# Four cross-attention layers in one kernel: constant rows replicated by transfer, preparation steps in a new order, epsilon as a tile, no shift column

## The chip, the cores and the metric

The kernel runs on one core of one Trainium2 chip. The metric is device time in microseconds, as the median of several executions. TensorE (PE), VectorE (DVE), ScalarE (ACT) and GpSimd (POOL) compute; SyncE (SP) issues all DMA transfers.

## The reference

Input are x (64 batches, 128 tokens, 256 features), a context ctx (64, 128, 128) and a side input (64, 128, 128), all float32. Four residual layers follow each other:

```
L0: x = x + softmax((x Wq + bq)(ctx Wk + bk)' / 16) (ctx Wv + bv) Wo + bo
L1: t = x + cross(ln(x), ln(ctx)) + cross(ln(x), ln(side));  x = t + ln(t) fc_W + fc_b
L2: p = x + softmax over the queries((x Wq + bq)(ctx Wk + bk)' / 16) (ctx Wv + bv);  x = ln(p) gamma + beta
L3: as L0, with its own weights
```

ln(x) is (x - mean) * (var + eps)^(-1/2) over the features, with eps 1e-5 in L1 and 1e-6 in L2; in L1 it has gains and offsets (g1, b1 for queries, g2, b2 for keys).

## The kernel before

**Groups.** The work is cut into 32 groups of two batches. Each group goes through some ninety steps such as `hi_L0`, `Q_L0`, `S_L0`, `max_L0`, `exp_L0`, `PT_L0`, `O_L0`, `OUT_L0`, `out_L0`, `stats_ln1`. A step belongs to one engine and handles a whole group. Below, `Q_L0(1)` is step `Q_L0` of group 1.

**Order.** A table sets the order on every engine. `STARTS` gives each step a number, `COMES` an offset for each group; `PREPARATIONS` gives numbers to the one-time work on the weights. `timetable()` sorts all of it, and each engine issues its own steps in that order, each behind its semaphore waits. Nothing overtakes.

**Preparation.** Projections are folded once: for each attention `a` (L0, L1a, L1v, L3) PE forms `M_a` = Wq Wk' and `N_a` = Wv Wo (`products`), `m_a` from the query bias (`query_bias`) and `n_*` from the value and output biases (`output_bias`). ACT and DVE cut M and N into a high and a low fp32r part (`M_hi`, `M_lo`). A constant row (an output bias, beta, gamma, a key gain) comes as one row of the tile `rows` on a single partition, and is spread over the partitions by a product with `ones_row` (L355, L395, L411, L419, L441): ten such products in all. ACT copies results out of PSUM into `bias_*` and `gamma_row`; DVE multiplies the keys' weights by the gain in PSUM (L869).

**Layer norm.** DVE computes `stats` (L909), `mean_var` (L915) and `var_eps` = var + eps (L919). POOL raises it to -1/2 (`rstd`, L1076). DVE forms `shift` = -mean * rstd (L943), and POOL computes x * rstd + shift (`norm_*`, L1082). For the norm before fc neither shift nor normalised x is made.

**PSUM.** Eight banks are handed out by `seats()` in the order of the table, always the one whose last user is emptied first.

Of the kernel before, what the change touches and what calls it, by code (L numbers as in the profile page):

```python
# [78 lines left out]
PREPARED = {"keys_L1": [("gain_L1a", "gained_L1a"), ("gain_L1v", "gained_L1v")],  # L79
            "products_L0": [("M_L0", "M_lo_L0"), ("N_L0", "N_lo_L0")],  # L80
            "vectors_L0": [("m_L0", "m_col_L0"), ("n_L0", "bias_L0")],
            "products_L1": [("M_L1a", "M_lo_L1a"), ("N_L1a", "N_lo_L1a"), ("M_L1v", "M_lo_L1v"), ("N_L1v", "N_lo_L1v")],
            "vectors_L1": [("m_L1a", "m_col_L1a"), ("m_L1v", "m_col_L1v"), ("n_L1", "bias_L1")],
            "fc": [("n_fc", "bias_fc"), ("mean_fc", "centred_fc")],
            "L2": [("M_L2", "M_lo_L2"), ("k_L2", "k_bias2"), ("n_L2", "bias_L2v")],
            "products_L3": [("M_L3", "M_lo_L3"), ("N_L3", "N_lo_L3")],
            "vectors_L3": [("m_L3", "m_col_L3"), ("n_L3", "bias_L3"), ("gamma", "gamma_row")]}
# [24 lines left out]

def seats(table):

    at = {(name, g): n for n, (_, g, name) in enumerate(table)}
    held, seat = [None] * BANKS, {}
    for _, g, name in table:
        uses = PREPARED.get(name, []) if g < 0 else [(name, EMPTIED_BY[name])] if name in EMPTIED_BY else []
        for use, emptied in uses:
            n = min(range(BANKS), key=lambda b: -1 if held[b] is None else held[b][2])  # L120
            assert held[n] is None or held[n][2] <= at[name, g], f"no bank for {use} {g}"
            seat[use, max(g, 0)] = n, held[n] and held[n][:2]
            held[n] = emptied, max(g, 0), at[name, g] if g < 0 else at[emptied, g]
    return seat


def build(nc, ins, out):
    with ExitStack() as stack:  # L128
# [109 lines left out]
        for engine, signals in SIGNALS.items():  # L238
# [1 line left out]
            for n, name in enumerate(name for _, _, p in table for name in signals.get(p, [])):  # L240
# [988 lines left out]
```

## Time and profile before

| what | value |
|---|---|
| median of 3 runs | 613.43 us (612.94 to 614.08) |
| profiled execution, its own time | 613.34 us |
| span of the profile, first to last instruction | 611.5 us |
| granted PE clock, mean | 0.993 |
| PE busy | 582.3 us, 95% |
| DVE busy | 537.5 us, 88% |
| POOL busy | 520.0 us, 85% |
| ACT busy | 431.5 us, 71% |

All times in the rows are counted from the start of the span. 1.84 us of the profiled execution lie outside it. A matmul on float32 leaves two records in the trace, a matmul on fp32r one. Busy time of PE is of pipelined matmuls, so its share does not say how fast they follow each other; the starts in the timeline do.

### The profile page before, as it was taken

To read this page: it belongs to the slowest core of one execution; us is meant where nothing else is said; L and a number is where in the kernel's file an instruction comes from. 1 tells how busy PE (TensorE), PEld (TensorE's weight loads), DVE (VectorE), ACT (ScalarE), POOL (GpSimd) and SP (SyncE) were. 2 spreads that over 40 slices of the span, in tenths; PEclk is the share of its full clock that TensorE was granted. 3 is DMA by queue.
4 is the path that set the end of the run, shared out by engine and by line. 5 is a ranking of instruction groups with operands and counts; after the bars stand their busy time and mean duration, and the time that the engine had idled before them with its cause. 6 is when DMAs were issued, how large, how long until landed. Compare 5 with 4: busy or idle time off the path is not lost. (4 is left out here: it accounts for less than half of the span.)

```text
span 611.5 us, 16892 instructions
## 1 busy us (share of the span) xinstructions
PE 582.3 (95%) x4872; PEld 567.7 (93%) x4872; DVE 537.5 (88%) x1685; ACT 431.5 (71%) x1473; POOL 520.0 (85%) x694
## 2 busy tenths in 40 slices
PE   4889999899999999999999999999999999999985
PEld 4778999899999999999999999999999899999974
DVE  1457789999999999999999999999999999989993
ACT  2546967777777778778777777877876788677443
POOL 3268887898999999999999999999999999867763
PEclk9998999999999999999999999999999999999999
DMA  8512211003222211122222221112333020000012
GB/s 274 217 62 70 82 48 46 3 1 96 80 78 80 78 56 51 54 80 79 78 80 79 79 79 53 48 60 78 114 104 114 17 89 28 18 3 19 19 35 70
DMA packets 28076, 42.80 MB, mean 70 GB/s; under 512 B 2513, under 2 KB 19793, under 8 KB 27985
## 3 DMA queue, kind: packets, MB, share of 16 engines
q1 hardware_dynamic: 27986, 41.72, 20.6%
q8 instruction: 41, 0.67, 0.5%
q14 instruction: 49, 0.40, 0.2%
HBM read 33.32 MB, written 8.39 MB: 68 GB/s over the span
## 5 line engine op out<-in xcount | busy, mean ns | idle before, releaser
L720 ACT ACTIVATE prob_L<-bank,neg_max_L 128x128 f32<-128x128 f32 x320 | 114.1, 379 | 70.1 <-DVE neg_max_L L952 69.7
L1082 POOL TENSOR_SCALAR xhat_ln<-x,rstd_ln,shift_ln 128x256 f32<-128x256 f32 x128 | 71.1, 564 | 14.0 <-issue 7.4
L652 ACT ACTIVATE oT_hi_L<-bank 128x256 fp32r<-128x256 f32 (+1 forms) x128 | 55.9, 460 | 34.4 <-PE bank L476 34.4
L720 ACT ACTIVATION_READ_ACCUMULATOR prob_L<-bank,neg_max_L 128x1 f32 x320 | 69.1, 216 | 0.0
L952 DVE TENSOR_REDUCE neg_max_L<-bank 128x2 f32<-128x256 f32 (+1 forms) x128 | 59.0, 477 | 11.5 <-PE bank L470 11.1
L652 ACT ACTIVATE xT_hi_L<-bank 128x512 fp32r<-128x512 f32 (+1 forms) x96 | 59.5, 620 | 7.4 <-PE bank L448 7.1
L854 DVE TENSOR_TENSOR oT_lo_L<-bank,oT_hi_L 128x256 fp32r<-128x256 f32 (+1 forms) x128 | 58.7, 478 | 2.9 <-ACT oT_hi_L L652 2.8
L1076 POOL TENSOR_TENSOR rstd_ln<-var_eps_ln,minus_half 128x2 f32<-128x2 f32 x64 | 45.3, 708 | 12.6 <-DVE var_eps_ln L919 7.4
L1116 POOL TENSOR_TENSOR xT_lo_L<-x_in,xT_hi_L 128x512 fp32r<-128x512 f32 x32 | 41.0, 1282 | 12.2 <-ACT xT_hi_L L652 12.2
L652 ACT ACTIVATE probT_L<-bank 128x256 f32<-128x256 f32 (+1 forms) x96 | 47.4, 495 | 4.3 <-PE bank L454 4.1
L985 DVE TENSOR_TENSOR x<-bank,x_bias 128x512 f32<-128x512 f32 x64 | 43.8, 685 | 6.5 <-PE bank L489 4.3
L919 DVE TENSOR_SCALAR var_eps_ln<-mean_var_ln 128x2 f32<-128x2 f32 x64 | 46.7, 730 | 2.2
L909 DVE BATCH_NORM_STATS2 stats_ln<-x 128x6 f32<-128x256 f32 x128 | 47.7, 414 | 0.9
L454 PE MATMUL bank<-ident,prob_L 128*128 128x128 f32 x256 | 44.0, 274 | 1.9 <-DVE xT_lo_L L854 0.9
L854 DVE TENSOR_TENSOR xT_lo_L<-bank,xT_hi_L 128x512 fp32r<-128x512 f32 x64 | 43.5, 679 | 1.0 <-ACT xT_hi_L L652 1.0
L487 PE MATMUL bank<-N_hi_L,oT_hi_L 128*128 128x256 f32 x128 | 41.2, 322 | 3.1 <-issue 1.5
L803 ACT ACTIVATE prob_L<-prob_L,inv_total_L 128x128 f32<-128x128 f32 x128 | 42.2, 441 | 1.5 <-DVE inv_total_L L959 1.5
L1156 POOL TENSOR_TENSOR x_res<-x_res,bias_L 128x512 f32<-128x512 f32 x32 | 41.1, 1283 | 2.5
L470 PE MATMUL bank<-ctx_in,qT_L 128*128 128x128 f32 x256 | 39.1, 276 | 3.2 <-issue 2.1
L1154 POOL TENSOR_TENSOR x_res<-xhat_ln,gamma_row 128x512 f32<-128x512 f32 x32 | 41.3, 1291 | 0.0
L1139 POOL TENSOR_TENSOR x_bias<-x,bias_fc 128x512 f32<-128x512 f32 x32 | 41.2, 1289 | 0.0
L1132 POOL TENSOR_TENSOR x_bias<-x,bias_L 128x512 f32<-128x512 f32 x32 | 41.2, 1287 | 0.0
(217 smaller groups left out, 2390.9 us busy)
## 6 DMA issues: line engine op xcount, KB each, us to landing
x_in<-in_x SPq DMA_DIRECT2D x32, 512.0 KB, 4.2
ctx_in<-in_ctx SPq DMA_DIRECT2D x32, 256.0 KB, 4.3
out<-y SPq DMA_DIRECT2D x32, 256.0 KB, 2.2
side_in<-in_side SPq DMA_DIRECT2D x32, 128.0 KB, 2.5
WqT_L<-in_L_WqT SPq DMA_DIRECT2D x3, 256.0 KB, 4.3
Wo_L<-in_L_Wo SPq DMA_DIRECT2D x2, 256.0 KB, 4.7
WkT_L<-in_L_WkT SPq DMA_DIRECT2D x3, 128.0 KB, 4.1
WvT_L<-in_L_WvT SPq DMA_DIRECT2D x2, 128.0 KB, 4.0
```

Source lines behind the costliest of these rows:

```text
L454: last = tr(block(bank, b), src[:, b, :], ident[:])
L652: activation(to, of, ACT.Copy).then_inc(done[step], 1)
L720: last = activation(at(prob[k], g)[:, b, :], block(bank, b), ACT.Exp, bias=at(neg_max[k], g)[:, b:b + 1], accum_out=at(total[k], g)[:, b:b ...
L803: last = activation(p[:, b, :], p[:, b, :], ACT.Copy, scale=at(inv_total["L1"], g)[:, b:b + 1])
L854: dve.tensor_tensor(to, of, hi.bitcast(F32), ALU.subtract).then_inc(done[step], 1)
L909: last = dve.bn_stats(st[:, n, :], tile)
L919: dve.tensor_scalar(at(var_eps[k], g)[:], mv[:, :, 1], eps, None, ALU.add).then_inc(done[f"var_{k}"], 1)
L952: dve.tensor_reduce(at(neg_max[k], g)[:], scores, AX.X, ALU.max, negate=True).then_inc(done[f"max_{k}"], 1)
L985: dve.tensor_tensor(flat(at(to, g)), bank_of(use, g)[:], flat(at(add, g)), ALU.add).then_inc(done[step], 1)
L1076: pool.tensor_tensor(at(rstd[k], g)[:], at(var_eps[k], g)[:], minus_half[:, 0:n], ALU.pow).then_inc(done[f"rstd_{k}"], 1)
L1082: last = pool.tensor_scalar(at(to, g)[:, n, :], tile, at(rstd[k], g)[:, n:n + 1], at(shift[k], g)[:, n:n + 1], ALU.mult, ALU.add)
L1154: pool.tensor_tensor(at(x_res, g)[:], at(xhat["ln2"], g)[:], every(gamma_row), ALU.mult).then_inc(done["x_gamma"], 1)
```

## The change

1. **Constant rows by transfer.** Each constant row is read by a transfer that writes it to all 128 partitions (`replicated` in the SP program): ten transfers of 128 KB (64 KB for the two gains) in place of the one for `rows`. The ten products with `ones_row` go. DVE adds the row when it takes the bias out of PSUM (`bias_plus`); POOL adds rows that belong together (`rows_L1`, `rows_L3`) and multiplies the keys' weights by the gain (`gained`, before on DVE). Copies of `m_col` and `k_bias2` move from ACT to DVE.
2. **First weights first.** WqT and WkT of L0 are the first two transfers. Each pair of weights has a semaphore of its own, so `M_L0` waits for two transfers, where it waited for four.
3. **Preparation in single steps.** What were 14 entries in `PREPARATIONS` are now 84, each for one engine, with new numbers. L3's preparation (2794 to 3293 before) now stands at 940 to 1060, ahead of `PT_L0(0)`.
4. **Epsilon as a tile.** `var_eps` is a tensor_tensor add of a tile `epsilon` where it was a tensor_scalar add of an immediate.
5. **No shift.** POOL computes (x - mean) * rstd from `mean_var` and `rstd`. The 96 `shift` instructions of DVE go, and with them the hop POOL to DVE to POOL.

The order of all group steps other than `shift` is the same as before.

```diff
-PREPARATIONS = {"load_first": -50, "constants": -40, "keys_L0": 81, "products_L0": 284, "vectors_L0": 406,
-                "load_rest": 506, "keys_L1": 516, "products_L1": 626, "fc": 666, "L2": 968, "vectors_L1": 1238,
...
+PREPARATIONS = {"load_qk_L0": -50, "load_cols": -49, "load_vo_L0": -48, "load_rows_L0": -47, "constants": -40, "scaled": -39, "M_L0": 100,
...
-            def load_first():
-                sp.dma_start(cols[:], ins["cols"].rearrange("p (n t) -> p n t", t=T)).then_inc(weights["vectors"], 16)
-                sp.dma_start(rows[:], ins["rows"].rearrange("(o n) d -> o n d", o=1)).then_inc(weights["vectors"], 16)
-                weights_of("L0")
+            def replicated(to, r, what):
+                n, width = ROWS.index(r), to.shape[1]
+                sp.dma_start(to[:], ins["rows"][n:n + 1, 0:width].to_broadcast([P, width])).then_inc(weights[what], 16)
...
+            def product_M(a):
+                def of():
                     w = stage[a]
-                    pe.wait_ge(weights[a], ATTENTION_WEIGHTS)
+                    pe.wait_ge(weights[f"{a}_qk"], TWO)
                     if a in LN_KEYS:
                         prepared(pe, f"gained_{a}")
...
-                terms += [(ones_row[:], row(r)) for r in extra]
...
+            def bias_plus(key, to, use, added):
+                dve.tensor_tensor(to[:], bank_of(use)[:, 0:D], added[:], ALU.add).then_inc(done[key], 1)
...
-                dve.tensor_scalar(at(var_eps[k], g)[:], mv[:, :, 1], eps, None, ALU.add).then_inc(done[f"var_{k}"], 1)
+                if g == 0:
+                    prepared(dve, "constants")
+                dve.tensor_tensor(at(var_eps[k], g)[:], mv[:, :, 1], epsilon[eps][:, 0:len(tiles)], ALU.add).then_inc(done[f"var_{k}"], 1)
...
-            def shift_of(k):
-                def of(g):
-                    dve.wait_ge(done[f"rstd_{k}"], g + 1)
-                    earlier(dve, f"norm_{k}", g, len(shift[k]))
-                    dve.scalar_tensor_tensor(out=at(shift[k], g)[:], in0=at(mean_var[k], g)[:, :, 0], scalar=-1.0,
-                                             in1=at(rstd[k], g)[:], op0=ALU.mult, op1=ALU.mult).then_inc(done[f"shift_{k}"], 1)
...
+            def gained(a):
+                def of():
+                    pool.wait_ge(weights[f"{a}_qk"], TWO)
+                    pool.wait_ge(weights[f"gain_{a}"], ONE)
+                    w = stage[a]["WkT"]
+                    pool.tensor_tensor(w[:], w[:], gain[a][:].unsqueeze(1).to_broadcast([P, T, P]), ALU.mult).then_inc(done[f"gained_{a}"], 1)
...
-                    last = pool.tensor_scalar(at(to, g)[:, n, :], tile, at(rstd[k], g)[:, n:n + 1], at(shift[k], g)[:, n:n + 1],
-                                              ALU.mult, ALU.add)
+                    last = pool.tensor_scalar(at(to, g)[:, n, :], tile, at(mean_var[k], g)[:, n, 0:1], at(rstd[k], g)[:, n:n + 1],
+                                              ALU.subtract, ALU.mult)
```

**SP, just ahead of the first context.** `ctx_in` is the tile that `hi_ctx(0)` on ACT and `S_L0(0)` on PE wait for. Before, it is the 24th transfer:

```order
L318 DMA fcW<-in_fc_W 128x2x256
L306 DMA WqT_L<-in_L_WqT 128x2x256
L306 DMA WkT_L<-in_L_WkT 128x2x128
L306 DMA WvT_L<-in_L_WvT 128x2x128
L306 DMA Wo_L<-in_L_Wo 128x2x256
L328 DMA ctx_in<-in_ctx 128x512
```

Now it is the 33rd (`row_L_bo`, `row_L_b` and `gamma_row` are the replicated rows of L3):

```order
L463 DMA WvT_L<-in_L_WvT 128x2x128
L463 DMA Wo_L<-in_L_Wo 128x2x256
L467 DMA row_L_bo<-in_rows 128x256
L467 DMA row_L_b<-in_rows 128x256
L467 DMA gamma_row<-in_rows 128x256
L509 DMA ctx_in<-in_ctx 128x512
```

All ten new transfers stand ahead of it, and the one for `rows` is gone: nine more. One of the ten (`row_L_bo` of L0) stands even ahead of the first `x_in`, which stays the seventh transfer.

**ACT, around `hi_ctx(0)`** (`ctxT_hi<-ctx_in`). Before, it stands behind everything that ACT does for L1v:

```order
L652 ACTIVATE M_L1v<-bank 128x256
L664 ACTIVATE M_hi_L1v<-bank,scaled_cols 128x128
L665 ACTIVATE M_hi_L1v<-bank,scaled_cols 128x128
L652 ACTIVATE N_L1v<-bank 128x256
L674 ACTIVATE N_hi_L1v<-bank,cols 128x256
L652 ACTIVATE ctxT_hi<-ctx_in 128x256
```

Now L1v stands behind it:

```order
L867 ACTIVATE N_hi_L1a<-bank,cols 128x256
L835 ACTIVATE ctxT_hi<-ctx_in 128x256
L835 ACTIVATE M_L1v<-bank 128x256
L849 ACTIVATE M_hi_L1v<-bank,scaled_cols 128x128
L850 ACTIVATE M_hi_L1v<-bank,scaled_cols 128x128
L835 ACTIVATE N_L1v<-bank 128x256
```

So PE's `m_L1v`, which needs the copy `M_L1v`, now comes behind the landing of the first context.

**PE, ahead of `PT_L0(0)`** (`prob_L_0`). Before, the products of L1's output bias with their two rows stand there:

```order
L395 MATMUL bank<-Wo_L1a,rep_bv_L1a 128x256 x2
L395 MATMUL bank<-N_L1a,rep_b_L1a 128x256
L395 MATMUL bank<-Wo_L1v,rep_bv_L1v 128x256 x2
L395 MATMUL bank<-N_L1v,rep_b_L1v 128x256
L395 MATMUL bank<-rows,ones_row 128x256 x2
L454 MATMUL bank<-ident,prob_L_0 128x128 x2
```

Now L3's four products (M, N, m, n) are the last ahead of it:

```order
L539 MATMUL bank<-WkT_L,WqT_L 128x128 x4
L550 MATMUL bank<-Wo_L,WvT_L 128x256 x2
L566 MATMUL bank<-scaled_cols,WkT_L 128x1 x2
L566 MATMUL bank<-scaled_cols,M_L 128x1 x2
L582 MATMUL bank<-Wo_L,rep_bv_L 128x256 x2
L636 MATMUL bank<-ident,prob_L_0 128x128 x2
```

## Rows read from the trace of the kernel before

**Rows 1.** The page: busy time, share of the span, instructions.
```profile
PE 582.3 (95%) x4872; PEld 567.7 (93%) x4872; DVE 537.5 (88%) x1685; ACT 431.5 (71%) x1473; POOL 520.0 (85%) x694
```

**Rows 2.** Windows: busy us and records by engine, granted clock, DMA share, GB/s.
```profile
300.00:350.00 50.00, 50.00 (x437) 49.84 (x437) 47.88 (x155) 37.80 (x131) 47.44 (x62) 1.00 0.23 73
...
13.24:18.20 4.96, 4.52 (x31) 4.11 (x31) 1.97 (x7) 2.45 (x8) 0.88 (x4) 1.00 1.07 385
...
29.85:33.26 3.41, 3.41 (x9) 2.29 (x8) 0.00 (x0) 0.00 (x0) 0.89 (x1) 0.50 0.09 36
...
50.30:53.72 3.42, 3.42 (x17) 3.42 (x17) 1.36 (x3) 0.77 (x3) 3.23 (x7) 0.50 0.55 208
```

**Rows 3.** Waits of PE over the span: who for whom, us, times, longest.
```profile
PE bank L487 <- DVE oT_lo_L L854: 3.4, 4, 1.4
...
PE bank L463 <- DVE xT_lo_L L854: 2.0, 3, 1.1
```

**Rows 4.** Timeline of PE: start, us, instructions, and idle before them.
```profile
7.39 2.04 PE L366 MATMUL bank<-WkT_L,WqT_L 128*128 128x128 f32 x8 [7.39 <-DMA Wo_L<-in_L_Wo]
...
32.49 1.49 PE L395 MATMUL bank<-rows,ones_row 1*128 1x256 f32 x4
33.91 0.44 PE L454 MATMUL bank<-ident,prob_L 128*128 128x128 f32 x2
...
42.46 1.06 PE L366 MATMUL bank<-WkT_L,WqT_L 128*128 128x128 f32 x8
...
44.03 0.47 PE L487 MATMUL bank<-N_hi_L,oT_hi_L 128*128 128x256 f32 x1
...
46.80 0.61 PE L381 MATMUL bank<-scaled_cols,WkT_L 128*128 128x1 f32 x4 [0.33 <-DVE M_lo_L L873]
...
50.24 1.17 PE L476 MATMUL bank<-probT_L,ctx_in 128*128 128x128 f32 x4
51.06 0.56 PE L463 MATMUL bank<-xT_hi_L,M_hi_L1a 128*128 128x256 f32 x1
```

**Rows 5.** Groups of DVE by line: busy us, mean ns, idle before.
```profile
L919 DVE TENSOR_SCALAR var_eps_ln<-mean_var_ln 128x2 f32<-128x2 f32 x64 | 46.7, 730 | 2.2
...
L943 DVE SCALAR_TENSOR_TENSOR shift_ln<-mean_var_ln,rstd_ln 128x2 f32<-128x2 f32 x64 | 15.4, 240 | 1.9 <-POOL rstd_ln L1076 1.9
...
L919 DVE TENSOR_SCALAR var_eps_keys<-mean_var_keys 128x4 f32<-128x4 f32 x32 | 14.9, 465 | 1.1
...
L943 DVE SCALAR_TENSOR_TENSOR shift_keys<-mean_var_keys,rstd_keys 128x4 f32<-128x4 f32 x32 | 6.4, 201 | 0.0
```

**Rows 6.** Line L919: duration ns min/median/max, first and last start.
```profile
L919 DVE TENSOR_SCALAR var_eps_ln<-mean_var_ln x64: 168/664/1393, 41.5 to 594.4; 128x2 f32<-128x2 f32 x64
```

**Rows 7.** Timelines of POOL and DVE around two short DVE instructions.
```profile
341.25 1.28 POOL L1116 TENSOR_TENSOR xT_lo_L<-x_in,xT_hi_L 128x512 fp32r<-128x512 f32 x1
...
341.28 1.27 DVE L919 TENSOR_SCALAR var_eps_ln<-mean_var_ln 128x2 f32<-128x2 f32 x1
...
36.58 1.26 POOL L1116 TENSOR_TENSOR xT_lo_L<-x_in,xT_hi_L 128x512 fp32r<-128x512 f32 x1
...
36.73 1.14 DVE L943 SCALAR_TENSOR_TENSOR shift_keys<-mean_var_keys,rstd_keys 128x4 f32<-128x4 f32 x1
```

**Rows 8.** Timeline of DVE, 42 to 50 us.
```profile
42.51 0.68 DVE L943 SCALAR_TENSOR_TENSOR shift_ln<-mean_var_ln,rstd_ln 128x2 f32<-128x2 f32 x1 [0.74 <-POOL rstd_ln L1076]
...
49.12 0.67 DVE L854 TENSOR_TENSOR xT_lo_L<-bank,xT_hi_L 128x512 fp32r<-128x512 f32 x1
```

**Rows 9.** The first group's timeline: SP issues its context, POOL computes lo_L0(0).
```profile
12.82 0.47 SPq L328 DMA_DIRECT2D ctx_in<-in_ctx  x1
...
10.97 1.27 POOL L1116 TENSOR_TENSOR xT_lo_L<-x_in,xT_hi_L 128x512 fp32r<-128x512 f32 x1 [7.27 <-ACT xT_hi_L L652]
```

**Rows 10.** Tile WqT_L, 0 to 4 us: issue to landing.
```profile
DMA to landing us min/median/max: 2.7/2.7/2.7
```

**Rows 11.** Tile ctx_in, 0 to 26 us: issue to landing of three.
```profile
DMA to landing us min/median/max: 5.2/6.1/6.9
```

More of the change, by code:

```diff
@@ L77 @@
               "S_L3": "exp_L3", "PT_L3": "pT_L3", "O_L3": "oT_lo_L3", "OUT_L3": "out_L3"}
[L79 to L87, printed above, removed]
@@ L88 @@
-SMALL = [f"{what}_{k}" for what in ("stats", "mean", "var") for k in ("keys", "ln1", "lnf", "ln2")] + ["x_gamma"]
-SIGNALS = {"TensorE": {"keys_L1": ["gain_L1a", "gain_L1v"], "products_L0": ["M_L0", "N_L0"], "vectors_L0": ["m_L0", "n_L0"],
[13 rows of a table removed]
+EMPTIED_BY |= {"m_L0": "m_col_L0", "n_L0": "bias_L0", "m_L1a": "m_col_L1a", "m_L1v": "m_col_L1v", "n_L1": "bias_L1", "n_fc": "bias_fc",
+               "mean_fc": "centred_fc", "M_L2": "M_lo_L2", "k_L2": "k_bias2", "m_L3": "m_col_L3", "n_L3": "bias_L3"}
+EMPTIED_BY |= {f"{w}_{a}": f"{w}_lo_{a}" for w in "MN" for a in ATTENTIONS}
@@ new lines @@
+OF_ENGINE = {"TensorE": [f"{w}_{a}" for w in "MNm" for a in ATTENTIONS] + ["n_L0", "n_L1", "n_L3", "n_fc", "mean_fc", "M_L2", "k_L2"],
+             "ScalarE": ([f"{w}_hi_{a}" for w in "MN" for a in ATTENTIONS] + [f"M0_{a}" for a in ("L1a", "L1v", "L3")]
+                         + ["N0_L1a", "N0_L1v", "gained_fc", "F_hi", "M_hi_L2", "Wv2_hi"]),
+             "VectorE": (["scaled"] + [f"{w}_lo_{a}" for w in "MN" for a in ATTENTIONS] + [f"m_col_{a}" for a in ATTENTIONS]
+                         + ["bias_L0", "bias_L1", "bias_L3", "bias_fc", "centred_fc", "F_lo", "M_lo_L2", "k_bias2", "Wv2_lo"]),
+             "GpSimd": ["constants", "gained_L1a", "gained_L1v", "rows_L1", "rows_L3"] + [f"rep_{a}" for a in ATTENTIONS + ["fc"]]}
@@ L106, in timetable @@
+SMALL = [f"{what}_{k}" for what in ("stats", "mean", "var") for k in ("keys", "ln1", "lnf", "ln2")] + ["x_gamma", "zeroed"]
 def timetable():
-    table = [(STARTS[name] + COMES[g], g, name) for name in STARTS for g in range(GROUPS)]
-    table += [(PREPARATIONS[name], -1, name) for name in PREPARATIONS]
+    table = [(times[g], g, name) for name, times in STARTS.items() for g in range(GROUPS)]
+    table += [(time, -1, name) for name, time in PREPARATIONS.items()]
     return sorted(table)
@@ L117, in seats @@
     for _, g, name in table:
[L118 to L123, printed above, removed]
+        if name in EMPTIED_BY:
+            n = min(range(BANKS), key=lambda b: -1 if held[b] is None else at[held[b]])
+            assert held[n] is None or at[held[n]] <= at[name, g], f"no bank for {name} {g}"
+            seat[name, g] = n, held[n]
+            held[n] = EMPTIED_BY[name], g
     return seat
@@ L188, in build @@
             layer_buffers(k)
-        stats, mean_var, var_eps, rstd, shift = ({} for _ in range(5))
+        stats, mean_var, var_eps, rstd = ({} for _ in range(4))
         for k, n in {"keys": A["L1"] * GROUP, "ln1": GROUP, "lnf": GROUP, "ln2": GROUP}.items():
@@ L212, in build @@
             Wv2 = sb("Wv2", [P, D], where=staging)
-            rows = sb("rows", [1, len(ROWS), D], where=staging)
+            rows = {r: sb(f"row_{r}", [P, D], where=staging) for r in ("L0_bo", "L1a_bo", "L1v_bo", "L3_bo", "L3_b1", "fc_bias")}
+            gain = {a: sb(f"gain_{a}", [P, P], where=staging) for a in ("L1a", "L1v")}
             for a in ATTENTIONS + ["fc"]:
@@ L237, in build @@
         times = {}
[L238 removed]
+        for engine, names in OF_ENGINE.items():
             raised = stack.enter_context(nc.semaphore(f"prepared_{engine}"))
[L240 removed]
+            for n, name in enumerate(name for _, g, name in table if g < 0 and name in names):
                 done[name], times[name] = raised, n + 1
@@ L413, in fc, with of @@
-            def fc():
-                pe.wait_ge(weights["fc"], FC_WEIGHTS)
+                def of():
+                    prepared(pe, "scaled")
+                    pe.wait_ge(weights[f"{a}_qk"], TWO)
+                    if a in LN_KEYS:
+                        prepared(pe, f"gained_{a}")
+                    bank = bank_for(pe, f"m_{a}")
+                    terms = [(stage[a]["WkT"][:, h, :], col(f"{a}_bq", h, scaled_cols)) for h in range(T)]
+                    if a in LN:
+                        prepared(pe, f"M0_{a}")
+                        terms += [(M0[a][:, t, :], col(f"{a}_b1", t, scaled_cols)) for t in range(T)]
+                    for n, (stationary, moving) in enumerate(terms):
+                        last = mm(bank[:, 0:1], stationary, moving, start=n == 0, stop=n == len(terms) - 1)
+                    last.then_inc(done[f"m_{a}"], 1)
@@ new lines, in query_bias, with output_bias, of @@
+                return of
+            def output_bias(key, attentions):
+                def of():
+                    bank = bank_for(pe, f"n_{key}")
+                    terms = []
+                    for a in attentions:
+                        prepared(pe, f"rep_{a}")
+                        pe.wait_ge(weights[f"{a}_vo"], TWO)
+                        terms += [(rep[a]["bv"][:, h, :], stage[a]["Wo"][:, h, :]) for h in range(T)]
+                        if a in LN_KEYS:
+                            prepared(pe, f"N0_{a}")
+                            terms += [(rep[a]["b2"][:], N0[a][:])]
+                    for n, (stationary, moving) in enumerate(terms):
+                        last = mm(bank[:, 0:D], stationary, moving, start=n == 0, stop=n == len(terms) - 1)
+                    last.then_inc(done[f"n_{key}"], 1)
+                return of
@@ L415, in fc, with n_fc @@
+            def n_fc():
+                pe.wait_ge(weights["fc"], ONE)
                 prepared(pe, "rep_fc")
                 bank = bank_for(pe, "n_fc")
-                terms = [(rep["fc"]["bv"][:, t, :], fcW[:, t, :]) for t in range(T)] + [(ones_row[:], row("fc_bias"))]
-                for n, (stationary, moving) in enumerate(terms):
-                    last = mm(bank[:, 0:D], stationary, moving, start=n == 0, stop=n == len(terms) - 1)
+                for t in range(T):
+                    last = mm(bank[:, 0:D], rep["fc"]["bv"][:, t, :], fcW[:, t, :], start=t == 0, stop=t == T - 1)
@@ L1067, in keys_L1, with replicated, of @@
-            def keys_L1():
-                replicated("L1a", "L1a_bv")
-                replicated("L1v", "L1v_bv")
+            def replicated(a):
+                def of():
+                    pool.wait_ge(weights["cols"], ONE)
+                    for t in range(T):
+                        last = pool.tensor_copy(rep[a]["bv"][:, t, :], col("fc_b" if a == "fc" else f"{a}_bv", t).to_broadcast([P, P]))
+                    if a in LN_KEYS:
+                        last = pool.tensor_copy(rep[a]["b2"][:], col(f"{a}_b2").to_broadcast([P, P]))
+                    last.then_inc(done[f"rep_{a}"], 1)
+                return of
@@ L1071, in rstd_of, with rows_L3 @@
+            def rows_L3():
+                pool.wait_ge(weights["rows_L3"], THREE)
+                pool.tensor_tensor(rows["L3_bo"][:], rows["L3_bo"][:], rows["L3_b1"][:], ALU.add).then_inc(done["rows_L3"], 1)
             def rstd_of(k, used_by):
                 def of(g):
+                    if g == 0:
+                        prepared(pool, "constants")
                     pool.wait_ge(done[f"var_{k}"], g + 1)
```

345 lines of the change are left out of this document (184 added, 161 removed), and 203 rows, old and new, of tables (COPIES, PREPARATIONS, SIGNALS, STARTS).

## The prediction, made before the changed kernel ran

> **What bounds the kernel now.** I read the page first. PE is busy 95%, DVE 88%, POOL 85% [rows 1], so three engines are close together and shares alone decide nothing. Next I took windows. In the middle of the run PE is busy 50.00 of 50 us, DVE 47.88, POOL 47.44 [rows 2]: PE never waits there. The 437 records in 50 us are one every 114 ns. The order of the group steps is unchanged, so the middle (about 100 to 450 us) can't get shorter by anything that DVE or POOL save. The time is PE's work, plus what PE loses at the start, in the fill of the pipeline and in the last groups. The list of PE's waits says who is late after the start: the two largest entries are DVE's `oT_lo` (3.4 us) and `xT_lo` (2.0 us) [rows 3]. The timeline of PE gives the landmarks of the start: first product at 7.39 us, behind the landing of the fourth weight tile; first softmax transposed (`PT_L0(0)`) at 33.91; first `Q_L1` at 51.06 [rows 4].
>
> **The change, part by part.**
>
> *First product.* `M_L0` now waits for the first two transfers alone. The first issue is at about 0.7 us, the next half a microsecond later; the tile WqT_L0 landed 2.7 us after its issue [rows 10]. So PE starts at about 0.7 + 0.5 + 2.7 = 3.9 us, 3.5 us earlier. I do not count that as gain: ACT's first steps need the first `x_in`, still the seventh transfer, and what PE does next is gated by POOL and by a transfer.
>
> *Gain multiply.* `gained_L1a` goes from DVE to POOL, behind `lo_L0(0)`, which ended at 10.97 + 1.27 = 12.24 [rows 9]. With about 0.3 us for the row put ahead of `x_in`, and 0.65 for a product half the size of that one, `M_L1a` starts near 13.2. PE, done with L0 by then, idles some 2.5 us. It hides in the 3.5 us gained.
>
> *Context.* This is the new gate. The 24th transfer was issued at 12.82 us [rows 9], that is one each 0.526 us from 0.7 on; the 33rd comes at 0.7 + 32 x 0.526 = 17.5. It landed 5.2 us after issue in a busy stretch [rows 11], where the DMA engines moved 385 GB/s at full share [rows 2]; a transfer into quiet queues took 2.7 [rows 10]. The ten rows add 8 x 128 + 2 x 64 = 1152 KB, at 385 GB/s 3 us; by bytes the old landing of 12.82 + 5.2 = 18.0 becomes 21.0. Bounds: 20.2 (quiet) and 22.7 (busy). I take 21.5, since the queues fall neither quiet nor stay full. The price of reading one row 128 times is in no row; see the rivals. `hi_ctx(0)` on ACT waits for it, the copy `M_L1v` is queued behind, and PE's `m_L1v` behind that: with two ACT steps of about 0.4 us, 22.4. PE will idle there about 4 us.
>
> *From there to `PT_L0(0)`.* PE has 68 records to issue: `m_L1v` 8, `n_L1` 12, `n_fc` and `mean_fc` 8, `M_L2` and `k_L2` 12, `S_L0(0)` 4, L3's four products 24. L3's M and N took 44.03 - 42.46 = 1.57 us for 12 records [rows 4], 0.13 each; 68 make 8.9, so 31.3. DVE's `m_col_L3` and `max_L0(0)` and ACT's two exponentials follow, some 1.3: 32.6. PE's clock was granted at half, 1.2 for 2.4 GHz, for 3.41 us of this stretch before and for 3.42 us from 50.30 on [rows 2], each costing 1.7 us of PE's work; two idles of 2.5 and 4 us just ahead make one such piece as likely as not, so half of 1.7. `PT_L0(0)` at 33.5: **gain 0.4** (bounds -3 and +3.5).
>
> The Trainium skill (TensorE: Matmul & The Clock Gate, Part 1: The HAM clock gate) says that the clock follows how busy PE has recently been. By it the longer idle would make the half clock certain, and the sum above 0.85 us worse.
>
> *PT to Q_L1(0).* Before, L3's preparation lay inside: 1.57 us at 42.46, and from 46.80 less its wait of 0.33 to 50.24, that is 3.77 [rows 4]. All 5.3 us leave this stretch. But PE can't use it all: `Q_L1(0)` needs `lo_L1(0)` of DVE, which ended at 49.12 + 0.67 = 49.79 [rows 8], so PE was the later by 1.27. Beyond that DVE's own chain must get shorter. It loses the `shift` at 36.73, 1.14 us long [rows 7], and the one at 42.51, 0.68 plus 0.74 of waiting for POOL [rows 8]: 2.56, of which `oT_lo` can use about 2.1, as ACT's `oT_hi` comes next. **Gain 1.3 + 2.1 = 3.4** (bounds 1.3 and 5.3).
>
> *Ten row products.* Two of them, as four records, took 33.91 - 32.49 = 1.42 us at half clock for the most part [rows 4]. Ten would be about 5 us of PE; seven lie ahead of `PT_L0(0)`, L3's three between the landmarks, and both stretches are costed above as a whole. No separate gain.
>
> *Shift.* DVE loses 96 instructions, 15.4 + 6.4 = 21.8 us [rows 5], 0.7 per group. In the middle they cover nothing, PE being late. If PE's idle in late groups came all from DVE, the gain were the 5.4 us of the two entries [rows 3]; I take 2.0, since several of those waits are the last groups' own latency, where PE, ACT and DVE hand over in turn. **Gain 2.0** (bounds 0 and 5.4).
>
> *Epsilon.* `var_eps` of 128x2 took 730 ns on average, 168 at least [rows 5, 6]. The timelines say why: at 341.28 it ran until 342.55, when POOL's tensor_tensor of 341.25 ended at 342.53 [rows 7]. It stands still while POOL runs. Will an add of two SBUF tiles escape? The removed `shift` is such an instruction, two SBUF tiles in, 128x4 out, and at 36.73 it ran until 37.87, when POOL's tensor_tensor of 36.58 ended at 37.84 [rows 7]. The same wait to 30 ns. So I cost this edit at **nothing** (bounds: 0 and 61.6 - 96 x 0.168 = 45 us of DVE time). POOL's side is covered too: `norm` keeps its size.
>
> The Trainium skill (SBUF — State Buffer, Who interferes with whom) speaks against this edit: a DVE instruction with two SBUF inputs contends with a GpSimd instruction that reads SBUF, as one in a 2-port mode does. The trace agrees for POOL's tensor_tensor, 1.14 and 1.27 us.
>
> *Copies to DVE, `rows_*` to POOL.* Below half a microsecond each, all in the start, in the terms above.
>
> Sum: 0.4 + 3.4 + 2.0 = 5.8 us. Span 611.5 - 5.8 = 605.7; with the 1.84 outside, 607.5. The profiled execution (613.34) is as good as the median (613.43), so **607.5 us** is the median too.
>
> **Rivals.**
>
> 1. *The epsilon add does escape POOL's lock* (15%). For it: the mean `shift` took only 240 and 201 ns [rows 5], so most did not wait. Against: the one at 36.73 did [rows 7], and `var_eps` stands in the table where POOL runs its long adds. DVE would shed up to 45 us; in the middle nothing follows, in fill and end the waits for DVE shrink by 3 more: 604.5.
> 2. *DVE does not hold the fill* (12%). PE keeps the 3.5 us of the earlier start or all 5.3 of L3's block: 607.5 less 5.3 - 3.4 = 1.9 and about 2 of the start: 603.6.
> 3. *Gain given back* (15%). What PE gains before 51 us it waits for later in the fill, where DVE and POOL are behind it: only the 2.0 and the 0.4 stay: 611.0.
> 4. *Slower: the first context comes late* (10%). The replicated rows all read one line of memory 128 times and stand ahead of `ctx_in(0)` in SP's queue. If they take three times what their bytes say, 6 us more, `ctx_in(0)` lands at 27.5, and PE idles 10 us behind `hi_ctx(0)`; every microsecond goes straight to `PT_L0(0)`. The forecast's 5.8 is gone once the landing is later than 27.3; with a second piece at half clock, 615. For it: the order above. Against: no transfer in rows 10 and 11 took over 6.9.
>
> **How the numbers follow.** The forecast has 48%, the rivals 15, 12, 15 and 10. Its own range is 605 to 610. A measurement of this kernel tells 0.2%, 1.2 us, from no change, so faster is below 612.2. The forecast, rivals 1 and 2 and most of rival 3 are faster: 84%. Rival 3's rest and the best of rival 4 are the same, 6%; slower 10%. The 80% range cuts rival 4 and the lower end of rival 2: 603.3 to 612.0.
>
> **What the profile after will show.** First matmul near 3.9 us; an idle of PE of about 4 us before `m_L1v`, ended by ACT and behind it by the landing of `ctx_in`; `PT_L0(0)` near 33.5; `Q_L1(0)` near 47.3; in the middle PE busy 50 of 50 as before and DVE down by about 2 us in 50; the `var_eps` group with a mean still over 0.5 us and single ones that end with a POOL tensor_tensor. The prediction is wrong if the `ctx_in` landing is far from 21.5, if `var_eps` shrinks to 0.2 us, or if the distance from `PT_L0(0)` to `Q_L1(0)` stays near 17.2.

## The result, and the profile after

The changed kernel takes 712.57 us (median of 4 runs, 711.19 to 713.51) against 613.66 us for the kernel before on the same chip: a ratio of 1.161, 95% interval 1.1585 to 1.1638. I had forecast 607.5 us, in a range of 603.3 to 612.0. The prediction was wrong, by 105 us, and in its direction.

The page of the kernel after, its part 1, which answers to [rows 1]:

```profile
PE 608.7 (86%) x4852; PEld 586.8 (82%) x4852; DVE 524.6 (74%) x1594; ACT 436.4 (61%) x1462; POOL 647.4 (91%) x699
```

POOL went from 520.0 to 647.4 us of work, with five instructions more. The shares of all other engines fell. PE's busy time rose by 26 us although it has 20 records fewer; part of the span now runs at the half clock (mean granted 0.956). The same window as in [rows 2], after:

```profile
300.00:350.00 50.00, 42.95 (x341) 41.84 (x340) 36.34 (x110) 30.40 (x108) 48.88 (x53) 0.93 0.20 66
```

PE waits 7 us in 50 there and did not wait at all before; POOL is busy 48.88 of the 50. PE's waits over the span, against [rows 3]:

```profile
PE bank L628 <- POOL xhat_ln L1299: 63.5, 33, 4.5
PE bank L669 <- DVE oT_lo_L L1026: 6.9, 10, 1.0
PE bank L539 <- POOL WkT_L1a L1275: 4.8, 1, 4.8
PE bank L566 <- ACT M_L1v L835: 4.0, 1, 4.0
```

One wait dominates: the transposes of the normalised tile wait for POOL's line 1299, the normalisation. Here are POOL's groups by line (busy us, mean ns, idle before), first of the kernel before:

```profile
L1082 POOL TENSOR_SCALAR xhat_ln<-x,rstd_ln,shift_ln 128x256 f32<-128x256 f32 x128 | 71.1, 564 | 14.0 <-issue 7.4 <-DVE shift_ln L943 6.5
...
L1082 POOL TENSOR_SCALAR keys<-side_in,rstd_keys,shift_keys 128x128 f32<-128x128 f32 x64 | 28.2, 451 | 0.0
L1082 POOL TENSOR_SCALAR keys<-ctx_in,rstd_keys,shift_keys 128x128 f32<-128x128 f32 x64 | 28.2, 450 | 8.7 <-DVE shift_keys L943 8.7
```

and of the kernel after:

```profile
L1299 POOL TENSOR_SCALAR xhat_ln<-x,mean_var_ln,rstd_ln 128x256 f32<-128x256 f32 x128 | 155.9, 1227 | 1.0 <-POOL rstd_ln L1293 0.8 <-issue 0.2
L1299 POOL TENSOR_SCALAR keys<-side_in,mean_var_keys,rstd_keys 128x128 f32<-128x128 f32 x64 | 50.6, 801 | 0.0
L1299 POOL TENSOR_SCALAR keys<-ctx_in,mean_var_keys,rstd_keys 128x128 f32<-128x128 f32 x64 | 50.5, 797 | 0.0
```

These are the same 256 instructions on the same shapes, each about twice as long: 257.0 us instead of 127.5, that is 129.5 us of POOL, 4.05 per group. The output's transfers give the period of a group. Before (SP's queue, the 6th and the 20th store that the view lists):

```profile
208.50 0.39 SPq L336 DMA_DIRECT2D out<-y  x1
...
446.50 0.40 SPq L336 DMA_DIRECT2D out<-y  x1
```

After, the same two:

```profile
236.97 0.40 SPq L517 DMA_DIRECT2D out<-y  x1
...
523.85 0.40 SPq L517 DMA_DIRECT2D out<-y  x1
```

Over 14 groups that is 17.00 us each before and 20.49 after. POOL's work per group was 47.44 / 50 x 17.00 = 16.1 us; with 4.05 more it is 20.2, above PE's 17.0. So POOL sets the pace. The 20.49 is a mean of periods between 18.8 and 22.3 us; in 7 of the 14 groups POOL also waits 0.8 us for DVE's `var_eps_lnf`. From the 3rd to the 21st store listed, 18 groups, it is 369.08 us against 307.60, so 61.5 of the 99.8 us by which the span grew lie there; 19.4 lie ahead of it and 18.9 behind it, where the pipeline fills and empties.

The start went wrong too, on a smaller scale. Landmarks of PE's timeline after, against [rows 4]:

```profile
3.78 2.07 PE L539 MATMUL bank<-WkT_L,WqT_L 128*128 128x128 f32 x8 [3.78 <-DMA WkT_L<-in_L_WkT]
...
13.38 2.04 PE L539 MATMUL bank<-WkT_L1a,WqT_L1a 128*128 128x128 f32 x8 [4.80 <-POOL WkT_L1a L1275]
...
24.49 0.99 PE L566 MATMUL bank<-scaled_cols,WkT_L1v 128*128 128x1 f32 x4 [4.00 <-ACT M_L1v L835]
...
39.24 0.44 PE L636 MATMUL bank<-ident,prob_L 128*128 128x128 f32 x2 [0.58 <-ACT prob_L L892]
...
54.90 0.58 PE L645 MATMUL bank<-xT_hi_L,M_hi_L1a 128*128 128x256 f32 x1 [0.96 <-DVE xT_lo_L L1026]
```

`PT_L0(0)` comes at 39.24 (forecast 33.5) and `Q_L1(0)` at 54.90 (forecast 47.3).

### The profile page after: what moved, and what is told of

Read it like the earlier page. It is cut to its first block and busy times, and to the rows that moved or that the text cites. A ratio compares the mean times of both kernels' runs of the same rounds, so it can differ in the third digit from the quotient of the medians.

```text
span 711.3 us, 16702 instructions
## 1 busy us (share of the span) xinstructions
PE 608.7 (86%) x4852; PEld 586.8 (82%) x4852; DVE 524.6 (74%) x1594; ACT 436.4 (61%) x1462; POOL 647.4 (91%) x699
## 3 DMA queue, kind: packets, MB, share of 16 engines
q1 hardware_dynamic: 29424, 42.89, 18.5%
## 5 line engine op out<-in xcount | busy, mean ns | idle before, releaser
L1299 POOL TENSOR_SCALAR xhat_ln<-x,mean_var_ln,rstd_ln 128x256 f32<-128x256 f32 x128 | 155.9, 1227 | 1.0 <-POOL rstd_ln L1293 0.8
L628 PE MATMUL bank<-ident,xhat_ln 128*128 128x128 f32 x256 | 44.6, 301 | 63.5 <-POOL xhat_ln L1299 63.5
L835 ACT ACTIVATE xT_hi_L<-bank 128x512 fp32r<-128x512 f32 (+1 forms) x96 | 58.0, 604 | 62.3 <-PE bank L628 62.1
L628 PEld LDWEIGHTS bank<-ident,xhat_ln 128*128 128x128 f32 x256 | 30.6, 150 | 70.3 <-POOL xhat_ln L1299 69.9
L892 ACT ACTIVATION_READ_ACCUMULATOR prob_L<-bank,neg_max_L 128x1 f32 x320 | 65.9, 206 | 0.0
L1026 DVE TENSOR_TENSOR oT_lo_L<-bank,oT_hi_L 128x256 fp32r<-128x256 f32 (+1 forms) x128 | 58.9, 479 | 4.7 <-ACT oT_hi_L L835 4.3
L835 ACT ACTIVATE probT_L<-bank 128x256 f32<-128x256 f32 (+1 forms) x96 | 44.3, 462 | 11.9 <-PE bank L636 11.5
L1299 POOL TENSOR_SCALAR keys<-side_in,mean_var_keys,rstd_keys 128x128 f32<-128x128 f32 x64 | 50.6, 801 | 0.0
L1299 POOL TENSOR_SCALAR keys<-ctx_in,mean_var_keys,rstd_keys 128x128 f32<-128x128 f32 x64 | 50.5, 797 | 0.0
L1342 POOL TENSOR_TENSOR x_bias<-x_in,bias_L 128x512 f32<-128x512 f32 x32 | 41.5, 1296 | 0.0
```

Of the source, the lines that this page charges most:

```text
L628: last = tr(block(bank, t * GROUP + b), src[:, b, t * P:(t + 1) * P], ident[:])
L835: activation(to, of, ACT.Copy).then_inc(done[step], 1)
L892: last = activation(at(prob[k], g)[:, b, :], block(bank, b), ACT.Exp, bias=at(neg_max[k], g)[:, b:b + 1], accum_out=at(total[k], g)[:, b:b ...
L1026: dve.tensor_tensor(to, of, hi.bitcast(F32), ALU.subtract).then_inc(done[step], 1)
L1299: last = pool.tensor_scalar(at(to, g)[:, n, :], tile, at(mean_var[k], g)[:, n, 0:1], at(rstd[k], g)[:, n:n + 1], ALU.subtract, ALU.mult)
L1342: pool.tensor_tensor(at(x_bias, g)[:], tile, every(bias["L0"]), ALU.add).then_inc(done["x_bias"], 1)
```

## The experiments

Theory N, formed from these lines: the loss is the duration of POOL's normalising instruction, and that comes from its form. Rival S: the reordered start and the replicated rows carry the loss, and the slow instruction is only a symptom of them. Within N, the form could be slow through its pair of operations (T1), through the mean being read with a stride (T2), or through contention (T3).

**One part at a time.** `e1_norm_alone` is the kernel before with this edit, and with the shift left out:

```diff
-  pool.tensor_scalar(at(to, g)[:, n, :], tile, at(rstd[k], g)[:, n:n + 1], at(shift[k], g)[:, n:n + 1], ALU.mult, ALU.add)
+  pool.tensor_scalar(at(to, g)[:, n, :], tile, at(mean_var[k], g)[:, n, 0:1], at(rstd[k], g)[:, n:n + 1], ALU.subtract, ALU.mult)
```

> The kernel before with one part of the change: normalisation as (x - mean) * rstd on POOL, no shift on DVE. Theory N (the loss sits in POOL's normalising instruction, which is slower in this form wherever it stands): the two norm groups take about 1227 and 800 ns as after, POOL gets some 4.0 us more per group of 17.0 us, of which it was busy 16.1, so the time is 700 to 715 us. Rival S (the loss comes from the reordered start and the replicated rows, and the slow norm instruction is a symptom of something there, such as where tiles lie): norm stays at 564 and 451 ns and the time is 611 to 614.

Measured: 711.03 us, ratio 1.156 (1.1505 to 1.162), the groups at 1224, 801 and 800 ns:

```profile
L1082 POOL TENSOR_SCALAR xhat_ln<-x,mean_var_ln,rstd_ln 128x256 f32<-128x256 f32 x128 | 155.8, 1224 | 1.0 <-POOL rstd_ln L1076 0.8 <-issue 0.2
```

Within its interval this one edit is the whole loss.

`e2_rest_alone` is the changed kernel with that edit undone and the shift back on DVE.

> The changed kernel with the shift put back on DVE and the normalisation as x * rstd + shift on POOL; all the rest of the change stays. Theory N: norm back at 564 and 451 ns, PE busy 50 of 50 us in the middle, and the time is that of before give or take what the start does. In the changed kernel PT_L0(0) came at 39.24 us, 5.3 later than before, with L3's 5.3 us of preparation already behind it, so the first Q_L1 should come near 51 and the time be 611 to 616 us. Rival S: 700 us or more.

Measured: 616.52 us, ratio 1.0011 (0.9987 to 1.0036), norm at 565 ns, PE 50.00 of 50 in the middle. Theory N holds, S falls. The rest of the change together is worth nothing that these runs can measure, where I had counted 3.8 us of gain without the shift.

`e3_eps_alone`:

```diff
-  dve.tensor_scalar(at(var_eps[k], g)[:], mv[:, :, 1], eps, None, ALU.add)
+  dve.tensor_tensor(at(var_eps[k], g)[:], mv[:, :, 1], epsilon[eps][:, 0:len(tiles)], ALU.add)
```

> The kernel before with one part of the change: epsilon added as a tile (tensor_tensor of two SBUF tiles) in place of a constant. My prediction's step: it stalls behind POOL's tensor_tensor as before, the three var_eps groups sum to about 71 us as before, 613 us, within 0.2%. Rival: the add escapes, the groups fall to 0.17 us each, 20 us in all, and the time to about 610.5.

Measured: ratio 1.0016 (0.9989 to 1.0043). The three groups:

```profile
L922 DVE TENSOR_TENSOR var_eps_ln<-mean_var_ln,epsilon 128x2 f32<-128x2 f32 x64 | 48.5, 758 | 2.3 <-DVE mean_var_ln L916 0.2
...
L922 DVE TENSOR_TENSOR var_eps_keys<-mean_var_keys,epsilon 128x4 f32<-128x4 f32 x32 | 13.4, 419 | 1.1
...
L922 DVE TENSOR_TENSOR var_eps_lnf<-mean_var_lnf,epsilon 128x2 f32<-128x2 f32 x32 | 9.2, 288 | 1.1
```

They sum to 71.1 us; before it was 46.7 + 14.9 [rows 5] + 9.6 for `lnf` = 71.2. In sum the add of two tiles takes as long as the add of a constant did.

**The form by itself.** `e4_forms` is the kernel before with a table of `tensor_scalar` forms on POOL behind the last group, each waiting for the one before it, with no other compute engine at work (620 to 756 us: nothing on PE, DVE or ACT).

> The kernel before, with a table of tensor_scalar forms run on POOL alone behind the last group (128, 256 and 512 elements wide, three times each); the added tail makes its total time meaningless. Theory T1 (the pair of operations sets the time): (subtract, mult) takes about 800 and 1227 ns at 128 and 256 whatever its scalars, (mult, add) 451 and 564. Theory T2 (the mean is read with a stride out of the mean/variance tile): only forms with the strided mean are slow, (mult, add) with it too. Theory T3 (contention with DVE): every form is fast here.

The groups of the table at 128x256 (busy us, mean ns). By line: 1177 (mult, add); 1180 (subtract, mult), its mean out of the mean/variance tile; 1183 the same with a compact mean; 1186 (mult, add) with the scalar out of that tile; 1189 (add, mult); 1192 (mult, subtract); 1195 (mult, mult); 1198 (add, add); 1201 (subtract, subtract); 1216 mult alone:

```profile
L1198 POOL TENSOR_SCALAR probe_out<-probe_in,probe_mean,probe_shift 128x256 f32<-128x256 f32 x3 | 3.7, 1237 | 0.3
L1201 POOL TENSOR_SCALAR probe_out<-probe_in,probe_mean,probe_shift 128x256 f32<-128x256 f32 x3 | 3.7, 1236 | 0.3
L1192 POOL TENSOR_SCALAR probe_out<-probe_in,probe_rstd,probe_shift 128x256 f32<-128x256 f32 x3 | 3.7, 1232 | 0.3
L1180 POOL TENSOR_SCALAR probe_out<-probe_in,probe_mean_var,probe_rstd 128x256 f32<-128x256 f32 x3 | 3.7, 1227 | 0.3
L1183 POOL TENSOR_SCALAR probe_out<-probe_in,probe_mean,probe_rstd 128x256 f32<-128x256 f32 x3 | 3.7, 1222 | 0.3
...
L1216 POOL TENSOR_SCALAR probe_out<-probe_in,probe_rstd 128x256 f32<-128x256 f32 x3 | 2.8, 930 | 0.3
...
L1186 POOL TENSOR_SCALAR probe_out<-probe_in,probe_mean_var,probe_shift 128x256 f32<-128x256 f32 x3 | 1.7, 558 | 0.3
L1189 POOL TENSOR_SCALAR probe_out<-probe_in,probe_mean,probe_rstd 128x256 f32<-128x256 f32 x3 | 1.7, 558 | 0.3
L1195 POOL TENSOR_SCALAR probe_out<-probe_in,probe_rstd,probe_shift 128x256 f32<-128x256 f32 x3 | 1.7, 557 | 0.3
L1177 POOL TENSOR_SCALAR probe_out<-probe_in,probe_rstd,probe_shift 128x256 f32<-128x256 f32 x3 | 1.7, 552 | 0.3
```

T1 holds: the pair of operations decides. T2 falls (1180 against 1183, 1186 against 1177), and T3 falls, since POOL was alone. There are two classes: (mult, add), (add, mult) and (mult, mult) at 552 to 558 ns, and (subtract, mult), (mult, subtract), (add, add), (subtract, subtract) at 1222 to 1237. What on POOL makes the difference no run shows.

**The change with a fast pair.** (add, mult) is fast, so the mean only has to come negated. DVE writes it beside var + epsilon in one instruction:

```diff
+  dve.scalar_tensor_tensor(out=at(var_eps[k], g)[:], in0=mv[:], scalar=eps, in1=signs[:, 0:len(tiles), :], op0=ALU.add, op1=ALU.mult)
-  ... at(mean_var[k], g)[:, n, 0:1], at(rstd[k], g)[:, n:n + 1], ALU.subtract, ALU.mult)
+  ... at(var_eps[k], g)[:, n, 0:1], at(rstd[k], g)[:, n:n + 1], ALU.add, ALU.mult)
```

`e5_add_mult` puts it into the changed kernel, `e6_before_add_mult` into the kernel before, where it measures the removal of the shift (together with a `var_eps` twice as wide, which this form needs).

> The changed kernel with one pair of operations exchanged: DVE writes the negated mean beside var + epsilon in one instruction (the mean is off by epsilon, 0.00001, in this form), and POOL normalises as (x + negated mean) * rstd. Nothing comes back of the shift. If the pair of operations is the whole loss in the middle: norm at 558 ns and 452 ns as in the table of forms, POOL 4 us less per group, PE 50 of 50 in the middle, and the start 3 us late as in the run with the shift put back; less my 2.0 for the shift, 612 to 616 us, a ratio of 0.997 to 1.002. If a normalisation with the mean costs more than its own duration (another wait for POOL or DVE in place of the shift): above 620 us.

> The kernel before, without the shift, with the same normalisation by the negated mean; start and loads as before. It measures what the removal of 96 DVE instructions is worth by itself. My term: 2.0 us (0 to 5.4), a ratio of 0.997 (1.000 to 0.991). Rival: DVE's own time is covered and nothing is gained, 1.000; DVE busy falls by about 20 us in both.

Measured: 617.11 us, 1.0036 (1.0017 to 1.0055), and 618.0 us, 1.0033 (1.0005 to 1.0061). The large loss is gone with one pair exchanged, as e5's group shows:

```profile
L1298 POOL TENSOR_SCALAR xhat_ln<-x,var_eps_ln,rstd_ln 128x256 f32<-128x256 f32 x128 | 69.8, 553 | 1.0 <-POOL rstd_ln L1292 0.8 <-issue 0.2
```

But both missed: e5 is a little above its range, and e6, where DVE has 14 us less work, is no faster than before, it is slower. The profiled execution of e6 (618.02 us) has a group every 17.28 us instead of 17.00, that of e5 one every 17.27; four of e6's ten timed executions took only 614 to 616 us, so the longer period need not stand in all of them. In e6's timelines of POOL and DVE:

```profile
320.22 1.29 POOL L1143 TENSOR_TENSOR x_bias<-x,bias_fc 128x512 f32<-128x512 f32 x1
321.61 1.02 POOL L1080 TENSOR_TENSOR rstd_keys<-var_eps_keys,minus_half 128x4 f32<-128x4 f32 x1
323.42 0.89 POOL L1080 TENSOR_TENSOR rstd_lnf<-var_eps_lnf,minus_half 128x2 f32<-128x2 f32 x1 [0.79 <-DVE var_eps_lnf L920]
...
320.49 1.04 DVE L920 SCALAR_TENSOR_TENSOR var_eps_keys<-mean_var_keys,signs 128x8 f32<-128x8 f32 x1
```

`var_eps_keys` starts 0.27 us behind POOL's 128x512 add and stands still until that ends (321.53 against 321.51). It passes the delay on to `var_eps_lnf`, and POOL waits 0.79 us for that one, in each of the 14 groups between 209 and 451 us, in e5 too. Before, it started 0.2 us ahead of that add and took 0.27 (timelines of POOL and DVE before):

```profile
318.50 1.29 POOL L1139 TENSOR_TENSOR x_bias<-x,bias_fc 128x512 f32<-128x512 f32 x1
...
318.29 0.27 DVE L919 TENSOR_SCALAR var_eps_keys<-mean_var_keys 128x4 f32<-128x4 f32 x1
```

To test it I moved the add (`e10_add_mult_swap`, the only edit against e6, in the table of starts):

```diff
-  ... "x2_bias": 6092, ...
+  ... "x2_bias": 6122, ...
```

> The kernel before with the normalisation by the negated mean and no shift (its period was 17.27 us against 17.00), and on POOL the 128x512 add x2_bias stands behind rstd_keys instead of ahead of it. Theory C (without the shift DVE's var_eps_keys falls into that add, stalls 1.04 us instead of 0.27, and delays var_eps_lnf, for which POOL then waits 0.79 us in every group): the stall goes, the period is back at 17.0 and the time at that of before, ratio 0.996 to 1.000. Rival (the longer period comes from the wider instruction of 8 columns or from the missing wait itself): the period stays at 17.27 and the ratio at 1.003.

Measured: ratio 0.9996 (0.9975 to 1.0017). In its timelines:

```profile
320.16 1.02 POOL L1080 TENSOR_TENSOR rstd_keys<-var_eps_keys,minus_half 128x4 f32<-128x4 f32 x1 [0.48 <-DVE var_eps_keys L920]
321.15 1.29 POOL L1143 TENSOR_TENSOR x_bias<-x,bias_fc 128x512 f32<-128x512 f32 x1
...
319.92 0.17 DVE L920 SCALAR_TENSOR_TENSOR var_eps_keys<-mean_var_keys,signs 128x8 f32<-128x8 f32 x1
```

The stall is gone and the period is back at 16.98 us. The collision was the cause of the longer period; the ratios of e6 and e10 alone would not show it, as their intervals overlap.

**A third of the dose.** `e9_third_dose` is the kernel before with the slow pair for `ln2` alone (64 of the 256 instructions, a third of the added time), the shift kept.

> The kernel before, where only the 64 normalisations of ln2 take the slow form (x - mean) * rstd on POOL; the shift is still computed for all, so that POOL's load is the only difference. POOL gets 2 x 0.665 = 1.33 us more per group, and was busy 16.15 of 17.0 us. If POOL bounds as soon as its work exceeds the period: some 17.5 us per group with its short waits, half a microsecond more over about 28 groups, 14 us, a ratio near 1.02. If PE's work hides it: 1.000. If the slow instruction costs in another way than by its own duration (a third of the whole loss of 96 us): 32 us, 1.05.

Measured: 657.14 us, ratio 1.0694 (1.0663 to 1.0724), far above my 14 us. The period is 18.83 us: POOL's added 1.33 is not partly hidden by the 0.9 it had to spare, all of it and more shows. The timelines of e9 say in part why:

```profile
300.20 1.28 POOL L1129 TENSOR_TENSOR x_bias<-x_in,bias_L 128x512 f32<-128x512 f32 x1
301.44 1.28 POOL L1143 TENSOR_TENSOR x_bias<-x,bias_fc 128x512 f32<-128x512 f32 x1
...
304.63 0.70 POOL L1076 TENSOR_TENSOR rstd_lnf<-var_eps_lnf,minus_half 128x2 f32<-128x2 f32 x1 [0.79 <-DVE var_eps_lnf L919]
...
301.05 1.70 DVE L919 TENSOR_SCALAR var_eps_keys<-mean_var_keys 128x4 f32<-128x4 f32 x1
```

With POOL's phase moved, `var_eps_keys` stands still for 1.70 us under two of POOL's adds in a row, and POOL then waits 0.79 for the next one: the collision of e6 once more, on top. The count per group: 17.44 us of work on POOL (244.10 in 14 groups), 0.79 of this wait and 0.32 of waiting for `shift_keys`, which the kernel before has too, make 18.55 of the 18.83. What e9 would take without the collision was not tried.

**The start.** In e2 ACT's timeline shows what holds PE from 20 to 24.4 us:

```profile
16.80 0.47 ACT L872 ACTIVATE N_hi_L1a<-bank,cols 128x256 fp32r<-128x256 f32 x1
23.57 0.42 ACT L840 ACTIVATE ctxT_hi<-ctx_in 128x256 fp32r<-128x256 f32 x1 [6.30 <-DMA ctx_in<-in_ctx]
23.89 0.36 ACT L840 ACTIVATE M_L1v<-bank 128x256 f32<-128x256 f32 x1
```

PE had finished `M_L1v` at about 19 us; its copy stands behind the context's rounding in ACT's queue. Two edits of e2, each one number in the table of starts: `e7_ctx_early` issues the transfer earlier (`load_ctx(0)` from 580 to 510.5), `e8_act_order` leaves it and moves ACT's `hi_ctx(0)` from 640 to 725, behind the copies of L1v.

> The changed kernel with the shift put back, and with the first context transfer issued 13 transfers earlier, right behind the L1v weights (issue near 10.3 us instead of 18.3). If the late landing is what holds the start: landing near 16, PE's idle of 4.4 us ahead of m_L1v goes, PT_L0(0) comes at about 34 instead of 39.1, Q_L1(0) at 50 to 51 instead of 54.1, and the ratio is 0.005 to 0.008 below that of the run with the shift put back (1.001). If other work holds the start (DVE's chain, the number of PE's records): PT_L0(0) earlier but the ratio within 0.002 of it.

> The changed kernel with the shift put back; transfers stay, but on ACT the first context rounding (hi_ctx(0)) stands behind the copies and roundings of L1v instead of ahead of them. If it is the place in ACT's queue that carries the late landing to PE: M_L1v is copied at about 19.2 us, PE goes on with m_L1v and n_L1 without the idle, and the gain is as with the early transfer, PT_L0(0) near 34 to 35. If the landing itself matters (q_L0, lo_ctx, S_L0 need it too): PT_L0(0) stays above 37.

Measured: 0.9936 (0.9908 to 0.9964) and 0.9934 (0.9909 to 0.9959), with `PT_L0(0)` at 34.23 and 32.65 us, against 39.06 in e2. The context still lands at 23.6 us in e8:

```profile
19.08 0.38 ACT L840 ACTIVATE M_L1v<-bank 128x256 f32<-128x256 f32 x1 [1.74 <-PE bank L544]
...
23.59 0.42 ACT L840 ACTIVATE ctxT_hi<-ctx_in 128x256 fp32r<-128x256 f32 x1 [2.89 <-DMA ctx_in<-in_ctx]
```

So the late landing as such costs nothing that these runs can measure; the place of `hi_ctx(0)` at the head of ACT's queue cost 0.77% of the time, 4.7 us (e2 against e8). Once that place is mended, the rest of the change with the shift kept is worth 0.7%.

`e11_gain_first` is e8 with POOL's gain multiply of L1a ahead of `lo_L0(0)`.

> The changed kernel with the shift put back and the first context rounding behind L1v's copies on ACT, and with POOL's gain multiply of L1a ahead of lo_L0(0) instead of behind it. M_L1a waited 2.9 us for it. If PE uses that: first M_L1a near 11 instead of 12.9, PT_L0(0) 1 to 2 us earlier than 32.65, ratio 0.990 to 0.992. If PE gives it back before PT_L0(0) (max and exp of group 0, and the half clock): 0.993 as with the order on ACT alone.

Measured: 0.9947 (0.9928 to 0.9966), no different from e8. `M_L1a` came only 0.4 us earlier, at 12.52, and `PT_L0(0)` at 32.76. What PE gains there is given back before `PT_L0(0)`.

`e12_all` joins the repairs: negated mean, `x2_bias` moved, ACT's order, gain first.

> The change with all repairs that the runs point to: normalisation by the negated mean, no shift, first context rounding behind L1v's copies on ACT, gain multiply ahead of lo_L0(0), x2_bias behind rstd_keys on POOL. If the collision is what the missing shift costs, 0.987 to 0.991, below the same start with the shift; if the missing shift costs in another way, 0.993 or more.

Measured: 608.83 us (606.81 to 608.89, 5 runs), ratio 0.9893 (0.9867 to 0.992), the fastest here and 1.1% faster than the kernel before. Its middle:

```profile
300.00:350.00 50.00, 50.00 (x439) 49.77 (x438) 47.08 (x145) 38.70 (x134) 47.48 (x63) 1.00 0.22 72
```

Against e11, which has the same start and the shift, the negated mean without the shift, with `x2_bias` moved, is worth 0.54%, 3.3 us. The profiles show where: `Q_L1(0)` comes at 45.36 us instead of 48.58, the 6th store at 202.04 instead of 205.27; from the 6th to the 20th store it is 237.8 us instead of 238.2, and behind that 165.2 instead of 164.9. So all but a few tenths are won ahead of `Q_L1(0)`.

## Why the prediction was wrong

**The failed step** is the last sentence on epsilon: "POOL's side is covered too: `norm` keeps its size." I took the duration of (mult, add) for (subtract, mult), an operation pair that no row of before showed, and put no bound on it. The instruction took 1227 ns instead of 564. That was worth 129.5 us of POOL and, as POOL had 0.9 us to spare per group, all of the loss within the interval of e1 (e1, e4, and e5, where it goes away). My step before it, that the middle can't get shorter, was true, but I never asked what could make it longer. None of the four rivals had this mechanism, and none of the three signs of being wrong looked at POOL.

**First product, gain multiply.** 3.78 and 13.38 us, forecast 3.9 and 13.2: right. That the late gain multiply hides was right too (e11). PE's idle ahead of it was 4.80 us, though, where I had 2.5, and PE then ran in part at the half clock (granted 0.64 from 13.0 to 18.5 us).

**Context.** The mechanism was right, the size was not: issue at 18.4 instead of 17.5, landing 5.2 us behind it where I had taken 4.0, rounding at 23.66 instead of 21.5, beyond my upper bound by 1 us. `m_L1v` followed at 24.49 (22.4). PE's idle there was 4.00 us, as forecast, but by luck: PE also came 2 us later than I had it. I had seen that `M_L1v` is queued behind `hi_ctx(0)`, and that is what cost the time (e8). Rival 4 has the mechanism, but the landing came 2.1 us later than forecast, not 6.

**`PT_L0(0)`.** 39.24 instead of 33.5. Of the 5.7 us, 2.1 are the landing. The stretch behind `m_L1v` took 14.75 instead of 11.1: after the idle PE ran at the half clock (granted 0.50 from 24.4 to 27.8 us, 0.58 to 31.2), and four records of `n_L1` took 2.05 us in after and e2, 1.11 in e8. e7, without the idle and with a granted clock of 1.00 throughout, took 11.67 us for the stretch. By this comparison the half clock cost some 3 us, where I had counted 0.85. The base was off as well: the profile before has `PT_L0(0)` at 33.91, but five other profiles with the same start have it at 36.5 to 41.4 (e9, e6, e10, e3, e1). The landmark that I started from was the earliest of six. At `Q_L1(0)` e2 stands at 54.14 us, the five at 52.7 to 58.9 and the profile before at 51.06; that fits e2 being only 0.1% slower in its timed runs, though 5.1 us later at `PT_L0(0)`.

**`PT_L0(0)` to `Q_L1(0)`.** Forecast 13.75 us. After: 15.66, with POOL's slow keys and `xhat` inside it. With a fast norm and no shift 13.03 (e5) and 13.21 (e12); with the shift 15.08 (e2). The term was right for the change as I had understood it, counted from the profile before.

**Shift.** Forecast 2.0 us of gain, nothing in the middle. Alone it gave a loss of 0.33% (e6), and neither gain nor loss with the collision out of the way (e10). The 3.3 us of e12 against e11 lie ahead of `Q_L1(0)`, where the term before this one had counted them already; behind it the 2.0 us did not show. The step that failed is "In the middle they cover nothing": less work on DVE and no wait for it on POOL moved the two against each other, into a stall.

**Epsilon.** The DVE side was right, to 0.1 us of 71 (e3).

The fair test of the other terms is e5, the change with a fast pair: 1.0036, where my 607.5 us was 0.9903, some 8 us apart. The ACT queue accounts for 4.7 of them. e12 comes to 0.9893, but with three orders changed that were not in the change; that this is so near 0.9903 is luck.

## What to carry to other kernels

An instruction whose pair of operations changes is a new instruction: measure it before any term is summed. A bound from what else runs at that size can be too low: the slowest 128x256 instruction on POOL in the profile before took 732 ns, the new one 1227. Ask of every engine how much it has to spare in the steady window (here 0.9 us per group of 17 on POOL) and what would use that up, not only what could be saved. Where two engines stall each other, taking work from one shifts its phase against the other, and a gain can turn into a stall; the late landing did harm here only through what stood behind it in the queue of the engine that waited.
